# A gated cross-attention block with top-1 experts: feature-major queries with LayerNorm's factor applied behind the product, and bias plus row maximum fused per head

## The chip, the cores and the metric

One NeuronCore of a Trainium2 chip. The metric is the device time of one execution in microseconds (us), lower is better. All arithmetic is in float32.

## The reference

128 sequences of 128 tokens with 256 features, 16 heads of 16 features. `bias` is a full score bias of 128 x 16 x 128 x 128 values, which is most of the memory traffic.

```
q  = lora(layernorm(x), Wq, bq, Aq, Bq)          # layernorm without affine part, eps 1e-5
k, v = lora(ctx, ...), lora(ctx, ...)
p  = softmax(q * 16**-0.5 @ k.T + bias)          # per sequence and head
x  = x + tanh(g_xattn) * (p @ v)
y  = layernorm(x)
e  = argmax(softmax(y @ Wg + bg))                # one of 8 experts per token
x  = x + tanh(g_ffn) * (gelu(y @ W1[e] + b1[e]) @ W2[e] + b2[e])
```

## The kernel before

It has two stages. The attention stage handles one sequence per step, in a software pipeline: the step of sequence n computes scores of n, finishes n-1 and n-2, and prepares sequences up to n+6. Each engine runs its own program (SP for loads, TensorE = PE, ScalarE = ACT, VectorE = DVE, GpSimd = POOL), in program order, and the engines meet by semaphores. Work that goes by pairs of sequences alternates: in an even step PE makes the query product for the pair n+2, n+3 (I call it a *query step*), in an odd step the key product for n+1, n+2 (a *key step*). Every fourth step adds the router's work for four sequences. The last stage runs the experts over tiles of 256 tokens and has no part in the change.

What one step does before the change, by engine:

- DVE: for each quarter of the 16 heads it adds the bias to the scores, from PSUM, into `sc` (`add_bias`, L1023, 128x512 elements); after two quarters a reduction over `sc` gives eight negated row maxima (`row_max`, L1029). Then, for the sequence n-2, the reciprocal of the softmax sums (L1119), the scaling of the output (L1123) and the residual (L1130); and the statistics of both LayerNorms (L1039 with L1052 for sequence n+5, L1044 with L1052 for n-2). In every fourth step `pick_experts` runs before the bias additions (L1057 to L1070), and in the step after it `list_slots` (L1075 to L1081).
- POOL: adds the negated maxima to `sc` in two halves (`subtract_max`, L455), makes `(var+eps)**-0.5` (L477, L479) and the shift `-mean*factor` for both norms (L484, twice), adds the value bias to `x_sb` (L492) and scatters a finished sequence (L510).
- ACT: exponentials (L862), the copy of the output (L856), both LayerNorms as one activation each (`normalise`, L849), evacuation of queries, keys, values and of two transposes (L829, L840, L904, L910, L917).
- PE: scores (L560), in key steps of every fourth kind the router product (L632), p @ v (L595), the transposes of the exponent's argument (`turn`, L585, in two groups of eight), of the output (L660), the query or key product (`project`, L611), the value product (L710), the transposes of the second norm's result (L724) and of the first's (L734), which give `XT`, the moving operand of the query product.

The semaphore `s_used` counts DVE's finished quarters. PE waits for the first two before the query or key product, since both write the banks of the scores (`b_s[0]`, `b_s[1]`), for the third before the value product (`b_v` is `b_s[2]`) and for the fourth before L724. Before its next scores PE waits only for ACT's evacuations and for `s_used` of the step before. The queries are evacuated by ACT out of `b_s[0:2]` within the query step. SP issues, in each step and in this order: the context of a pair in every second step (L357), x of sequence n+6 (L364), which waits for `x2_ok` (L1130), and two halves of the bias of n+3 (L373), which wait for the last transposes of n-1.

## Time and profile before

| | |
|---|---|
| median of 3 runs | 1283.33 us (1281.91 to 1287.55) |
| span of the profiled execution | 1282.7 us, by which all sums here are made |
| attention stage | from about 18 us to about 1004 us: 128 steps |
| busy of the span | PE 99%, DVE 86%, POOL 81%, ACT 67% |
| DMA | 263.5 MB, 205 GB/s |

In the profile L12 is line 12 of the kernel. PEld is the loading of weights into TensorE, which overlaps its products; the ends of products are modelled, so the starts of the weight loads say more of PE's pace than its busy share does. Several instructions of a kind that follow each other are merged to one row with a count.

### The profile page before, as it was taken

What the parts mean: (1) busy time and instruction counts of PE and PEld (TensorE: products, weight loads), DVE (VectorE), ACT (ScalarE), POOL (GpSimd) and SP (SyncE); (2) the same over time, 40 slices, a digit from 0 to 9 for tenths busy, and PEclk for the clock granted to TensorE, in tenths of its full rate; (3) what the DMA queues carried; (4) which work ended last, traced back from release to release, by engine and by line L of the source; (5) the groups of instructions that cost most, each with busy time, mean ns of one, the idle gap of its engine ahead of it and who ended that gap; (6) DMA issues with size and microseconds to landing.
All of it is one profiled execution on the core that took longest, in us unless ns stands there. A gap on an engine that the chain in (4) does not pass through costs nothing. (4 is left out here: it accounts for less than half of the span.)

```text
span 1282.7 us, 42229 instructions
## 1 busy us (share of the span) xinstructions
PE 1264.4 (99%) x12820; PEld 1078.7 (84%) x12820; DVE 1098.7 (86%) x2504; ACT 860.4 (67%) x1916; POOL 1034.5 (81%) x1179
## 2 busy tenths in 40 slices
PE   8999999999999999999999999999999999999997
PEld 7888888888888888888888888888887788888886
DVE  6899999999999999999999999999999856665655
ACT  4777777777777777777777777777776533333332
POOL 4879989999999999999999999989988755544545
PEclk9999999999999999999999999999999999999999
DMA  6655655556655656555555555555655589888885
GB/s 237 213 179 196 193 187 181 188 186 196 191 185 181 186 187 197 191 192 183 181 185 187 195 193 185 181 184 187 192 195 182 187 271 282 281 278 281 276 281 184
DMA packets 110649, 263.48 MB, mean 205 GB/s; under 512 B 15332, under 2 KB 34278, under 8 KB 110464
## 3 DMA queue, kind: packets, MB, share of 16 engines
q1 hardware_dynamic: 96912, 226.76, 56.6%
q0 software_dynamic: 12624, 34.62, 6.9%
q10 hardware_dynamic: 1056, 1.39, 0.3%
q8 instruction: 28, 0.46, 0.2%
q14 instruction: 29, 0.24, 0.1%
HBM read 226.72 MB, written 36.91 MB: 206 GB/s over the span
## 5 line engine op out<-in xcount | busy, mean ns | idle before, releaser
L455 POOL TENSOR_TENSOR sc<-sc,negmax 128x1024 f32<-128x1024 f32 x256 | 482.4, 1901 | 25.6 <-DVE negmax L1029 20.7
L1023 DVE TENSOR_TENSOR sc<-bank,sc 128x512 f32<-128x512 f32 x512 | 328.2, 683 | 12.3 <-PE bank L560 7.5
L1029 DVE TENSOR_REDUCE negmax<-sc 128x8 f32<-128x1024 f32 x256 | 312.4, 1220 | 16.3
L862 ACT ACTIVATE PT<-bank 128x512 f32<-128x512 f32 x512 | 281.1, 607 | 1.7 <-PE bank L585 1.5
L585 PE MATMUL bank<-cst,sc 128*128 128x128 f32 x2048 | 272.6, 276 | 0.0
L585 PEld LDWEIGHTS bank<-cst,sc 128*128 128x128 f32 x2048 | 225.3, 140 | 25.8 <-issue 25.1
L525 POOL DMA_INDIRECT out<-og,ids x120 | 118.8, 990 | 114.7 <-issue 106.6
L856 ACT COPY OT<-bank 128x512 f32<-128x512 f32 x128 | 75.1, 587 | 152.1 <-PE bank L595 152.0
L510 POOL DMA_INDIRECT rows_dram<-x2n,slot_i x128 | 136.5, 1066 | 29.3 <-issue 25.2
L560 PE MATMUL bank<-KT,QT 32*128 32x256 f32 x2048 | 146.6, 400 | 0.6 <-ACT V L904 0.6
L595 PE MATMUL bank<-PT,V 128*32 128x128 f32 x4096 | 137.6, 275 | 0.3 <-issue 0.3
L710 PE MATMUL bank<-wv,CT 128*128 128x256 f32 x512 | 134.3, 385 | 0.0
L595 PEld LDWEIGHTS bank<-PT,V 128*32 128x32 f32 x4096 | 106.6, 110 | 32.1 <-ACT PT L862 27.2
L611 PE MATMUL bank<-XT,wq 128*128 128x256 f32 x512 | 125.3, 388 | 2.9 <-DVE sc L1023 2.4
L611 PE MATMUL bank<-CT,wk 128*128 128x256 f32 x512 | 125.6, 388 | 0.9 <-DVE sc L1023 0.9
L840 ACT ACTIVATE KT<-bank,bk_half,cst 128x256 f32<-128x256 f32 x256 | 123.9, 565 | 1.5 <-PE bank L611 1.5
L763 PE MATMUL bank<-xgT,w_sb 128*128 128x256 f32 (+1 forms) x552 | 123.1, 366 | 0.4 <-DMA w_sb<-in_w 0.3
L777 PE MATMUL bank<-CT,hT 128*128 128x256 f32 x516 | 122.6, 379 | 0.7 <-DVE og L1238 0.7
L560 PEld LDWEIGHTS bank<-KT,QT 32*128 32x128 f32 x2048 | 92.5, 184 | 25.0 <-issue 21.2
L1238 DVE SCALAR_TENSOR_TENSOR og<-bank,tg,QT 128x512 f32<-128x512 f32 x64 | 45.9, 717 | 78.2 <-DMA out<-og,ids 56.6
L710 PEld LDWEIGHTS bank<-wv,CT 128*128 128x128 f32 x512 | 94.2, 191 | 19.9 <-DVE sc L1023 5.3
L777 PEld LDWEIGHTS bank<-CT,hT 128*128 128x128 f32 x516 | 97.1, 190 | 13.8 <-issue 1.1
(148 smaller groups left out, 2052.0 us busy)
## 6 DMA issues: line engine op xcount, KB each, us to landing
sc<-in_bias SPq DMA_DIRECT2D x256, 512.0 KB, 4.9
w_sb<-in_w SPq DMA_DIRECT2D x69, 257.0 KB, 3.9
CT<-in_w SPq DMA_DIRECT2D x69, 256.0 KB, 4.1
xg<-rows_dram SPq DMA_DIRECT2D x63, 272.0 KB, 3.8
x_sb<-in_x SPq DMA_DIRECT2D x128, 128.0 KB, 2.0
CT<-in_ctx_in SPq DMA_DIRECT2D x64, 256.0 KB, 5.4
rows_dram<-x2n,slot_i POOLq DMA_INDIRECT x128, 3.8
out<-og,ids POOLq DMA_INDIRECT x120, 4.0
```

Source lines behind the costliest of these rows:

```text
L455: nc.gpsimd.tensor_tensor(s, s, m, ALU.add).then_inc(sub_ok, 1)
L510: nc.gpsimd.indirect_dma_start(rows_dram, bass.IndirectOffsetOnAxis(ap=slot_i[:, g, j:j + 1], axis=0), x2n[:, t.slot(8), :], None).then_in ...
L560: ins = mm(b_s[j][:, 2 * P * c:2 * P * c + 2 * P], QT[rows, pair, c, P * sq:P * sq + P], KT[rows, pair, c, sq].rearrange("p e k -> p (e k) ...
L585: ins = nc.tensor.transpose(turn_bank(t, q)[:, P * h:P * h + P], sc[:, t.slot(4), o:o + P], ident)
L595: ins = mm(b_x[CELL * j:CELL * j + CELL, P * (h // 4):P * (h // 4) + P], V[:, t.slot(8), h, :], PT[:, t.slot(2), P * h:P * h + P], start=T ...
L611: ins = mm(b_s[o][:, 0:2 * P], W[w][:, c, o * P:o * P + P], moving[:, c, :], start=(c == 0), stop=(c == KC - 1))
L710: ins = mm(b_v[:, 0:HID], CT[:, pair, c, tok:tok + P], W["v"][:, c, :], start=(c == 0), stop=(c == KC - 1))
L777: ins = mm(y_half, hT[:, t.slot(2), c, a * P:a * P + P], w2_of(t)[:, c * HID:c * HID + HID], start=(c == 0), stop=(c == KC - 1))
L840: ins = nc.scalar.activation(KT[:, pair, o, :, e, :], b_s[o][:, 0:2 * P].rearrange("p (s k) -> p s k", s=2), ACT.Identity, bias=bk_half[:, ...
L862: nc.scalar.activation(PT[:, t.slot(2), 512 * q:512 * q + 512], turn_bank(t, q)[:], ACT.Exp).then_inc(pt_ready, 1)
L1023: nc.vector.tensor_tensor(s, b_s[q][:], s, ALU.add).then_inc(s_used, 1)
L1029: nc.vector.tensor_reduce(negmax[:, t.slot(2), 8 * h:8 * h + 8], sc[:, t.slot(4), 1024 * h:1024 * h + 1024].rearrange("p (h k) -> p h k", ...
```

## The change

1. The query product takes raw x, laid out feature-major by the host (`x_turned`) and loaded into `XT` by one DMA per pair. The first `normalise`, the PE transposes L734 and the copy L917 go. The subtraction of the mean is folded into the query weights at set-up (each weight column less its mean). LayerNorm's factor, one number per token, is multiplied in behind the product: SP writes POOL's column of 128 factors to DRAM (`send_scale`) and reads it back as a row spread over 128 partitions (`spread_scale`) into `RS`; DVE multiplies the product by `RS` into `QT` (`scale_queries`), and ACT adds the query bias in place.
2. Bias addition and row maximum become one `tensor_tensor_reduce` per head on DVE, 128x128 elements with an accumulated maximum, 16 per step. POOL subtracts the maxima.
3. The value product moves to bank `b_x`, so its wait for `s_used` goes. PE waits for `scaled_ok` before the scores of a key step. POOL makes one shift instead of two.

```diff
@@ sync
+            def send_scale(t):
+                sp.wait_ge(rs_ok, t.n(1, 1))
+                sp.dma_start(rs_dram[t.n()], ln[:, (t.k - 7) % 8, 0, 0:1]).then_inc(rs_out, 16)
+            def spread_scale(t):
+                if t.reached(4):
+                    sp.wait_ge(scaled_ok, t.per(2, 1, -1))
+                sp.wait_ge(rs_out, t.n(16, 16))
+                sp.dma_start(RS[:, pair, tok:tok + P], rs_rows[t.n()].partition_broadcast(P)).then_inc(rs_in[pair], 16)
             def step(i, k):
+                behind = seq(i, k, -4)
+                if behind and not (isinstance(i, int) and k < 0):
+                    send_scale(behind)
...
-                        sp.wait_ge(xn_ok, t.n(1, -7))
+                if behind and behind.slot(2) == 0:
+                    if behind.reached(4):
+                        sp.wait_ge(q_ready, behind.per(2, KC, -KC))
+                    sp.dma_start(XT[:, behind.k // 2 % 2], x_turned[behind.per(2)]).then_inc(xT_in[behind.k // 2 % 2], 16)
+                if behind:
+                    spread_scale(behind)
@@ gpsimd
-                nc.gpsimd.tensor_tensor(s, s, m, ALU.add).then_inc(sub_ok, 1)
+                nc.gpsimd.tensor_tensor(s, s, m, ALU.subtract).then_inc(sub_ok, 1)
@@ tensor
                 if cur:
                     pe.wait_ge(v_evac, val.n() if val else N)
+                    if ky and ky.slot(2) == 0:
+                        pe.wait_ge(scaled_ok, ky.per(2, 1, 1))
...
-                    if cur:
-                        pe.wait_ge(s_used, cur.n(4, 3))
-                    elif val.reached(1):
+                    if not cur and val.reached(1):
...
-                if nxt:
-                    pe.wait_ge(xn_ok, nxt.n(1, 1))
-                    for c in range(KC):
-                        ins = nc.tensor.transpose(b_x[:, c * P:c * P + P],
-                                                  xn[:, nxt.slot(2), c * P:c * P + P], ident)
-                    ins.then_inc(xt_ready, 1)
@@ scalar, queries(t), now the last work of a query step
+                act.wait_ge(scaled_ok, t.per(2, 1, 1))
                 for o in range(KC):
-                    act.wait_ge(q_ready, t.per(2, KC, o + 1))
-                    ins = nc.scalar.activation(QT[:, pair, o, :], b_s[o][:, 0:2 * P],
+                    ins = nc.scalar.activation(QT[:, pair, o, :], QT[:, pair, o, :],
                                                ACT.Identity, bias=bq_col[:, o:o + 1])
@@ vector
                 dve.wait_ge(s_ready, t.n(4, q + 1))
-                s = sc[:, t.slot(4), 512 * q:512 * q + 512]
-                nc.vector.tensor_tensor(s, b_s[q][:], s, ALU.add).then_inc(s_used, 1)
-            def row_max(t, h):
-                nc.vector.tensor_reduce(
-                    negmax[:, t.slot(2), 8 * h:8 * h + 8],
-                    sc[:, t.slot(4), 1024 * h:1024 * h + 1024].rearrange("p (h k) -> p h k", h=8),
-                    AX.X, ALU.max, negate=True).then_inc(max_ok, 1)
+                for h in range(4 * q, 4 * q + 4):
+                    s = sc[:, t.slot(4), P * h:P * h + P]
+                    ins = nc.vector.tensor_tensor_reduce(
+                        out=s, in0=b_s[q][:, P * (h % 4):P * (h % 4) + P], in1=s, scale=1.0, scalar=LOWEST,
+                        op0=ALU.add, op1=ALU.max, accum_out=rowmax[:, t.slot(2), h:h + 1])
+                ins.then_inc(s_used, 1)
...
+            def scale_queries(t):
+                dve.wait_ge(rs_in[pair], t.per(4, 32, 32))
+                for o in range(KC):
+                    dve.wait_ge(q_ready, t.per(2, KC, o + 1))
+                    ins = nc.vector.tensor_tensor(QT[:, pair, o, :], b_s[o][:, 0:2 * P], RS[:, pair, :], ALU.mult)
+                ins.then_inc(scaled_ok, 1)
@@ vector, step: behind L1130 and ahead of L1044
+                        if qry and qry.slot(2) == 0:
+                            scale_queries(qry)
@@ vector, set-up: behind merge(2, "k")
+            dve.wait_ge(s_setc, 1)
+            nc.vector.scalar_tensor_tensor(
+                out=W["q"][:], in0=bank[SETUP_BANKS[1]][:, 0:HID].unsqueeze(1).broadcast_to([P, KC, HID]),
+                scalar=-1.0 / HID, in1=W["q"][:], op0=ALU.mult, op1=ALU.add).then_inc(s_setd, 1)
```

## Rows read from the trace of the kernel before

**Rows 1.** The page, part 1: busy us (share of the span) and instructions by engine.
```profile
PE 1264.4 (99%) x12820; PEld 1078.7 (84%) x12820; DVE 1098.7 (86%) x2504; ACT 860.4 (67%) x1916; POOL 1034.5 (81%) x1179
```
**Rows 2.** Busy time in four consecutive steps: stage, length, busy, clock, DMA share, GB/s.
```profile
500.55:508.66 8.11, 8.11 (x103) 7.03 (x103) 7.60 (x16) 6.47 (x16) 7.56 (x9) 1.00 0.54 170
508.66:516.26 7.60, 7.60 (x88) 6.49 (x87) 7.18 (x16) 5.46 (x13) 6.79 (x9) 1.00 0.65 208
...
sum 30.85, PE 30.85 PEld 26.15 DVE 28.75 ACT 23.58 POOL 28.07; mean PE 7.71 PEld 6.54 DVE 7.19 ACT 5.90 POOL 7.02
```
**Rows 3.** Timeline of PE's weight loads: start, duration, then the idle time before.
```profile
508.66 0.74 PEld L560 LDWEIGHTS bank<-KT,QT 32*128 32x128 f32 x16 [0.17 <-issue]
...
514.97 0.25 PEld L734 LDWEIGHTS bank<-cst,xn 128*128 128x128 f32 x2
515.18 0.90 PEld L585 LDWEIGHTS bank<-cst,sc 128*128 128x128 f32 x8
516.26 0.74 PEld L560 LDWEIGHTS bank<-KT,QT 32*128 32x128 f32 x16 [0.17 <-issue]
...
529.03 0.73 PEld L710 LDWEIGHTS bank<-wv,CT 128*128 128x128 f32 x4 [0.22 <-DVE sc L1023]
```
**Rows 4.** Timeline of DVE over the same steps.
```profile
499.54 0.25 DVE L1119 RECIPROCAL rden<-bank 128x16 f32<-128x16 f32 x1
...
501.71 1.29 DVE L1023 TENSOR_TENSOR sc<-bank,sc 128x512 f32<-128x512 f32 x2
...
508.90 0.19 DVE L1057 TENSOR_REDUCE lmax<-L 128x4 f32<-128x32 f32 x1
...
510.54 1.29 DVE L1023 TENSOR_TENSOR sc<-bank,sc 128x512 f32<-128x512 f32 x2
...
515.63 0.25 DVE L1119 RECIPROCAL rden<-bank 128x16 f32<-128x16 f32 x1
...
516.53 0.42 DVE L1130 TENSOR_TENSOR x<-bank,x_sb 128x256 f32<-128x256 f32 x1
517.05 0.43 DVE L1044 BATCH_NORM_STATS2 st<-x 128x6 f32<-128x256 f32 x1
...
518.28 1.28 DVE L1023 TENSOR_TENSOR sc<-bank,sc 128x512 f32<-128x512 f32 x2
```
**Rows 5.** The page, part 5: groups by line, count, busy us, mean ns.
```profile
L1023 DVE TENSOR_TENSOR sc<-bank,sc 128x512 f32<-128x512 f32 x512 | 328.2, 683 | 12.3 <-PE bank L560 7.5
L1029 DVE TENSOR_REDUCE negmax<-sc 128x8 f32<-128x1024 f32 x256 | 312.4, 1220 | 16.3
```
**Rows 6.** Timeline of DVE in the set-up: small instructions with no input.
```profile
16.92 0.07 DVE L1001 MEMSET terms<- 128x18 f32 x1
16.94 0.07 DVE L1002 MEMSET upto<- 128x9 f32 x1
```
**Rows 7.** Timeline of an early step in which DVE waits for the scores.
```profile
31.86 0.74 PEld L560 LDWEIGHTS bank<-KT,QT 32*128 32x128 f32 x16 [0.17 <-issue]
...
33.10 0.69 DVE L1023 TENSOR_TENSOR sc<-bank,sc 128x512 f32<-128x512 f32 x1 [1.00 <-PE bank L560]
```
**Rows 8.** Timeline of POOL: the same instruction in two consecutive steps.
```profile
521.64 3.75 POOL L455 TENSOR_TENSOR sc<-sc,negmax 128x1024 f32<-128x1024 f32 x2
...
526.71 0.50 POOL L484 TENSOR_SCALAR x2n<-x2n,mv 128x1 f32<-128x1 f32 x2 [0.18 <-POOL x2n L479]
...
529.18 3.75 POOL L455 TENSOR_TENSOR sc<-sc,negmax 128x1024 f32<-128x1024 f32 x2
```
**Rows 9.** Timeline of SP's DMA issues.
```profile
508.41 0.33 SPq L364 DMA_DIRECT2D x_sb<-in_x  x1
509.06 0.85 SPq L373 DMA_DIRECT2D sc<-in_bias  x2
```
**Rows 10.** The page, part 6: DMA issues, count, KB each, us to landing.
```profile
sc<-in_bias SPq DMA_DIRECT2D x256, 512.0 KB, 4.9
...
x_sb<-in_x SPq DMA_DIRECT2D x128, 128.0 KB, 2.0
```
**Rows 11.** Timeline of the start-up, PE's weight loads and DVE.
```profile
10.95 0.69 DVE L991 SCALAR_TENSOR_TENSOR wk<-bank,wk 128x512 f32<-128x512 f32 x1
...
11.40 1.59 PEld L611 LDWEIGHTS bank<-XT,wq 128*128 128x128 f32 x8 [0.76 <-ACT XT L917]
```

More of the change, by code:

```diff
@@ L39 @@
 TO_FT = float(3 << 30)
+LOWEST = -3.4028234663852886e38
 CELL = 32
@@ L548, in _ @@
             pe.wait_ge(s_id, 16)
+            pe.wait_ge(s_cst, 16)
+            pe.wait_ge(s_setd, 3)
+            for c in range(KC):
+                ins = mm(bank[SETUP_BANKS[1]][:, 0:HID], cst[:, C_ONE:C_ONE + P], W["q"][:, c, :],
+                         start=(c == 0), stop=(c == KC - 1))
+            ins.then_inc(s_setc, 1)
             def scores(t):
@@ L843, in keys, with normalise @@
                 ins.then_inc(k_evac, 1)
-            def normalise(t, n, row, rows, dst, done, turned):
-                act.wait_ge(shift_ok[n], t.n(1, 1))
+            def normalise(t):
+                row = t.slot(8)
+                act.wait_ge(shift_ok, t.n(1, 1))
                 if t.reached(2):
-                    act.wait_ge(turned, t.n(1, -1))
-                nc.scalar.activation(dst, rows, ACT.Identity, bias=ln[:, row, n, 1:2],
-                                     scale=ln[:, row, n, 0:1]).then_inc(done, 1)
+                    act.wait_ge(x2t_ready, t.n(1, -1))
+                nc.scalar.activation(xn2[:, row, :], x2[:, t.slot(2), :], ACT.Identity, bias=ln[:, row, 1, 1:2],
+                                     scale=ln[:, row, 1, 0:1]).then_inc(xn2_ok, 1)
             def copy_output(t):
@@ L1135, in step @@
                     aggregate(ahead, 0)
+                if qry and qry.slot(2) == 0 and not done:
+                    scale_queries(qry)
                 stats(done, 1)
```

110 lines of the change are left out of this document (52 added, 58 removed).

## The prediction

> **What bounds the kernel now.** I read the busy shares first: PE 99%, DVE 86%, POOL 81% [rows 1]. In the page's slices DVE stands at nine tenths until the expert stage begins and falls then, so the change acts on the attention stage alone: 128 steps, 32 groups of four. One group, at the full clock, takes 30.85 us [rows 2]. Then the timelines, to see who has slack. PE's weight loads follow each other densely; what is idle before them is 0.17 to 0.33 us at changes of tile shape, and one wait of 0.22 us for DVE in the group [rows 3]. DVE is just as dense: from the reciprocal to the next step's first bias addition is 2.17 us of instructions and their own hand-overs, and bias plus maximum takes 510.54 to about 515.6, 5.0 us [rows 4]. POOL's own round is 521.64 to 529.18, 7.54 us, against a mean step of 7.71 [rows 2, 8]. ACT has room: 5.90 of 7.71 [rows 2]. So three engines lie within about 2.5%. PE sets the pace, DVE has nearly nothing to spare, and POOL is next. Whatever the change takes from PE is gained only if DVE does not become slower by more than a few tenths per step.
>
> **PE.** Two transposes per step go. From the load of L734 to the next load is 514.97 to 515.18, 0.21 to 0.22 us [rows 3]; four times 0.22 is 0.88 us a group. PE's floor becomes 30.85 - 0.88 = 29.97 us. The 0.22 us wait [rows 3] disappears with the value product's new bank; I don't count it, since new waits of such a size are likely, and keep 29.75 as the lower end. Both products that stay wait for DVE's first two quarters as before.
>
> **DVE, the fused instruction.** Per step, four additions and two reductions of 4 x 683 + 2 x 1220 ns [rows 5], 5.0 us as they overlap, give way to 16 instructions of 128x128. Everything hangs on T, the time from start to start of two of them. No row shows this instruction. A neighbour with the same operands lasts 683 ns at 512 columns and 0.42 us at 256 [rows 4, 5], so about 1.03 ns a column and 0.287 us at 128 columns. Two additions with no wait between them take 1.28 us, where 2 x 0.683 would be 1.37 [rows 4, 5]: some 0.08 us of each hides under the next. That gives 0.205 us. Writing the accumulated maximum is a further small operation. Its nearest row is the memset, which has an output and no input and starts 0.02 us after the one before [rows 6]. I take T = 0.235 us. The lower end is 0.205 (the maximum for nothing). The upper end is no overlap and a full separate operation of the size of the router's smallest, 0.19 us [rows 4]: 0.48 us. I take the low value since the instructions have no waits between them, like the pair of additions, and the write is nearest to the memset. At that value the block takes 16T = 3.8 us instead of 5.0.
>
> The Trainium skill speaks on both terms. "VectorE: DVE Perf Modes", section "Two Vector instructions with no wait between them", counts an operation that writes out its accumulator as two instructions, of which the second has no input; no row here shows one, and by it there are 32 instructions in place of 16. The same page's "The DRAIN you can't avoid" and "Rules for kernel authors" say that the next operation doesn't begin until the pipe is empty, advise against fusing for speed and ask for a low count of operations. Against that stands this trace's overlap of 0.08 us in a pair [rows 4, 5]. By the rule the fused block would be the slower one; that is the first rival.
>
> **DVE, the scaling.** Once per pair, between L1130 and L1044, two 128x256 multiplications from PSUM come in, each 0.42 us like L1130, starting 0.34 us apart (0.42 - 0.08). They fill the hand-over between L1130 and L1044, 517.05 - 516.53 = 0.52 us, so they add about 0.6 us per pair. What is queued behind the wait for `q_ready` and `rs_in` on DVE is the statistics and then the next bias block. The query product is done long before L1130 ends, since the product lies before the value product, L724, L734 and L585 in PE's order.
>
> **The new meeting point.** PE may start the scores of a key step only when DVE has scaled. Before, DVE could trail by up to two us. So I cost pairs, from the scores of one key step to those of the next. The first bias instruction can begin 33.10 - 31.86 = 1.24 us after the scores' first load [rows 7]. In the query step, from the reciprocal to the end of scaling is (516.53 - 515.63) + 0.34 + 0.34 + 0.42 = 2.0 us [rows 4], 2.1 with the wake-up. The router's choice costs 510.54 - 508.90 = 1.6 us [rows 4] in one pair of two.
> - Pair with the router's work (8.11 + 7.60 us before [rows 2]): PE needs 15.71 - 0.44 = 15.27. The way through DVE is 1.24 + 16T + 2.17 + 1.6 + 16T + 2.1 = 7.1 + 32T: 14.6 at T = 0.235.
> - The other pair (30.85 - 15.71 = 15.14 before [rows 2]): PE needs 14.70. The way through the key step on PE and the query step on DVE is 7.39 + 1.24 + 16T + 2.1 = 10.7 + 16T: 14.5 at T = 0.235.
>
> Both stay under PE's time until T = 0.25, but only just. PE then sets the pace, with 29.97 us a group.
>
> **The rest, costed at nothing.** POOL loses one L484 in two, 0.25 us of 0.50 [rows 8], so its round is 7.3 us against a step of 7.49: covered, by 0.2 us, and it caps any further gain at 29.2 a group. ACT loses a normalisation and a copy. The query bias moves to the end of its query step and waits there for the scaling; behind it is queued the next step's output copy, which waits for p @ v anyway, and ACT has 1.8 us a step free [rows 2]. SP issues, per step, a 512-byte write, a spread read and half an XT load more, all ahead of the two bias loads. Its x load already waits for L1130, at 508.41, and the bias follows at 509.06 [rows 9]; 0.33 us for each issue moves the bias by under 1 us, and it has two steps of slack against 4.9 us to landing [rows 10]. The factor's write is issued at a step's start and may land behind 1 MB of bias, 4.9 us, still before that x load; the spread read goes out behind it and lands about 2 us later [rows 10], near 511 for the trace's step. The scaling that needs it comes at 516.9 [rows 4]: 5.7 us of cover. If that cover were gone, DVE would wait inside the meeting point. DMA is at 0.54 to 0.65 [rows 2] and moves some 12% more.
>
> **Start-up.** The query weights now wait for the key weights' merge, 10.95 + 0.69, one more merge and a scaling of about 1.1 us together: 12.8 instead of 11.40 [rows 11]. Scaling stands in front of the key product too. Bounds 0 and 4 us; I take 2.
>
> **The sum.** 1282.7 - 32 x 0.88 + 2 = 1256.5; the median stood 0.6 above the profiled span: 1257 us. With the wait on the value product gained too and no start-up cost: 1282.7 - 32 x 1.10 = 1247.5.
>
> **The rivals.**
> 1. *The fused instructions don't overlap.* T is then 0.287 or more, with a write that waits for its result 0.30 to 0.34. From T = 0.25 each further 0.01 us costs 0.48 us a group, and from T = 0.27 on the kernel is slower than before: 16.3 + 15.3 = 31.6 at 0.287, which gives 1309. At 0.30: 16.7 + 15.5 = 32.2, and 32 x 1.35 + 2 more than 1283: 1328. At 0.34: 18.0 + 16.4, 1397 (there the second pair goes through DVE twice, 5.5 + 32T). For it: a running maximum has to be complete before it is written, and no row shows such an instruction. Against: the pair of additions, the memsets. At the upper end, 0.48, it would be some 1680; I leave that out, since it stacks two worst cases. Chance 32%.
> 2. *PE's gain is spent at the meeting point.* With T of 0.255 to 0.275, or 0.3 to 0.4 us more of wake-ups per pair, the cycles through DVE take the 0.44 us per pair back: about 1282. For it: the two margins above are 0.2 and 0.7 us. Chance 14%.
> 3. *The factor comes late.* It decides when the round trip through DRAM exceeds about 8 us, from a step's start to 516.9. Two us too late would cost each of 64 pairs 2 us: 1385. The cover speaks against it. Chance 4%.
>
> **How the numbers follow.** The forecast case (PE sets the pace, 1247 to 1268) has 50%. Faster by over 0.5% is that case, 0.50; within 0.5%, about what a measurement of this kernel can tell from no change, is rival 2, 0.14; slower is rivals 1 and 3, 0.36, the other sign. The range reaches from the lower end, 1247, to 1360 (T about 0.32), which leaves out roughly the upper half of rival 1 and of rival 3. The likeliest case's own range is 1247 to 1268.
>
> **What would show it.** Right: 2048 fused instructions on DVE that start 0.22 to 0.25 us apart; L1023 and L1029 gone; a bias block of 3.6 to 4.0 us; DVE busy well under nine tenths of the attention stage; PE dense, with a group near 30 us and no wait for DVE before L560. Wrong: PE idle before L560 in key steps behind DVE's multiplication (rival 1 or 2, told apart by the start-to-start time), DVE idle before the multiplication behind a DMA into RS (rival 3), or SP's bias issues so late that DVE waits for them.

## The result, and the profile after

The changed kernel takes 2017.83 us (median of 4 runs, 2013.23 to 2019.98); the kernel before took 1284.24 beside it. The ratio is 1.570 [1.567, 1.574]. The prediction said 1257, between 1247 and 1360: the sign is wrong, and the range is missed by 658 us. The profiled execution has a span of 2016.1 us.

Page of the changed kernel: busy time by engine (answers [rows 1]), the chain that ended last, four groups of part 5 (count | busy us, mean ns | idle before, releaser), and one DMA issue (KB, us to landing).

```profile
PE 1390.3 (69%) x12568; PEld 1158.6 (57%) x12568; DVE 974.1 (48%) x5961; ACT 772.7 (38%) x1660; POOL 997.8 (49%) x1051
...
DMA 69%; PE 14%; SPq 9%; issue 6%; DVE 1%; ACT 0%; POOLq 0%; POOL 0%; DVEq 0%; ACTq 0%
...
L1042 DVE CUSTOM_DVE_ANT_0 sc<-bank,sc 128x128 f32<-128x128 f32 x2048 | 443.9, 286 | 264.3 <-PE bank L595 133.7
...
L595 PE MATMUL bank<-KT,QT 32*128 32x256 f32 x2048 | 195.6, 509 | 476.0 <-DVE QT L1101 443.9
...
L1052 DVE BATCH_NORM_STATS2 st<-x_sb 128x6 f32<-128x256 f32 x128 | 53.7, 419 | 399.6 <-DMA x_sb<-in_x 399.5
...
L1042 DVE DVE_READ_ACCUMULATOR2_ANT rowmax<- 128x1 f32 x2048 | 170.1, 83 | 0.3 <-issue 0.2
...
x_sb<-in_x SPq DMA_DIRECT2D x128, 128.0 KB, 11.1
```

No engine is the bound any more: PE fell from 99% to 69%, DVE from 86% to 48%. The chain is DMA for 69% of the span, and nearly all of that is one transfer: the next row of the page gives `rs_dram<-x2n`, the factor's write, 68%. PE is idle for 476 us ahead of the scores (L595), 444 of them behind DVE's scaling; DVE waits 400 us for x. The same 128 KB load of x that landed in 2.0 us [rows 10] takes 11.1. Who waits for the write is told by the waits of SP's queue from 100 to 1700 us (total us, times, longest) and by its issues in two steps (start, duration):

```profile
SPq L364 <- DMA rs_dram<-x2n: 1085.4, 117, 11.8
```

```profile
802.80 0.86 SPq L402 DMA_DIRECT2D sc<-in_bias  x2
804.38 0.36 SPq L356 DMA_DIRECT2D rs_dram<-x2n  x1
805.07 0.35 SPq L379 DMA_DIRECT2D CT<-in_ctx_in  x1
805.74 0.33 SPq L384 DMA_DIRECT2D x_sb<-in_x  x1
806.39 0.33 SPq L389 DMA_DIRECT2D XT<-in_x_turned  x1
815.20 0.33 SPq L366 DMA_DIRECT2D RS<-rs_dram  x1
815.87 0.86 SPq L402 DMA_DIRECT2D sc<-in_bias  x2
816.96 0.83 SPq L356 DMA_DIRECT2D rs_dram<-x2n  x1
818.04 0.58 SPq L384 DMA_DIRECT2D x_sb<-in_x  x1
828.73 0.33 SPq L366 DMA_DIRECT2D RS<-rs_dram  x1
829.38 0.86 SPq L402 DMA_DIRECT2D sc<-in_bias  x2
```

Each step has the same shape. SP issues the write (804.38), the loads of x, and then waits at L364 for the write to land, 10.8 us after its issue; only then go the spread read, the two bias loads and the next step's write, 1.8 us together. The next round is 816.96 to 828.73, 11.8 us. SP's own loop is 12.6 us long from the write at 804.38 and 13.5 from spread read to spread read (815.20 to 828.73), and the steps are 13.33 us apart in the mean (first score weight load of the first step at 37.57, of the 128th at 1730.4, over 127). In the kernel before they were 7.71 [rows 2]. They are not even: over steps 17 to 112, intervals of 17.1 and 9.6 us alternate in the mean, since PE waits for the scaling once in a pair, and two of SP's rounds go to a pair. The bias loads, which had nothing to do with the factor, stand behind its wait. The DMA engines don't carry a load meanwhile; their busy tenths in 40 slices of 815 to 829 us:

```profile
DMA  0009772893799489999997722000200000000000
```

From about 824 to 828.7 they are all but idle, while SP waits for the landing of the 512 bytes that it issued at 816.96. A window of 700 to 800 us (length; busy us and count of PE, PEld, DVE, ACT, POOL; granted clock, DMA share, GB/s):

```profile
700.00:800.00 100.00, 69.71 (x696) 57.66 (x696) 48.64 (x338) 42.00 (x90) 53.64 (x56) 0.80 0.60 128
```

The granted clock is 0.80 here, a mean of its two levels, where [rows 2] show full speed; a score product takes 509 ns in the mean instead of 400. PE is idle for 30 of the 100 us and waits for others, so I count the clock as a consequence of the waits and not as their cause; that is argued. `e2_no_factor_dma` below, without the factor's route, has a granted clock of 0.996 in the mean.

The fused instruction is as the prediction had it. DVE in one step (start, duration, the idle time before in brackets):

```profile
809.41 0.29 DVE L1042 CUSTOM_DVE_ANT_0 sc<-bank,sc 128x128 f32<-128x128 f32 x1 [1.05 <-PE bank L595]
809.63 0.08 DVE L1042 DVE_READ_ACCUMULATOR2_ANT rowmax<- 128x1 f32 x1
809.63 0.29 DVE L1042 CUSTOM_DVE_ANT_0 sc<-bank,sc 128x128 f32<-128x128 f32 x1
...
812.98 0.26 DVE L1137 RECIPROCAL rden<-bank 128x16 f32<-128x16 f32 x1
```

Two instructions per head, 286 and 83 ns, and the next head starts 0.21 us after the first: the 83 ns are hidden, and so is a part of the 286. Sixteen heads take 3.57 us to the reciprocal.

### The profile page after: what moved, and what is told of

It reads as the page before. It is cut to its first block, busy times and chain, and to the rows that moved or that the text cites. A ratio compares the mean times of both kernels' runs of the same rounds, so it can differ in the third digit from the quotient of the medians.

```text
span 2016.1 us, 45866 instructions
## 1 busy us (share of the span) xinstructions
PE 1390.3 (69%) x12568; PEld 1158.6 (57%) x12568; DVE 974.1 (48%) x5961; ACT 772.7 (38%) x1660; POOL 997.8 (49%) x1051
## 4 chain that ended last, share of the span: by engine, by line
DMA 69%; PE 14%; SPq 9%; issue 6%; DVE 1%; ACT 0%; POOLq 0%; POOL 0%; DVEq 0%; ACTq 0%
DMA rs_dram<-x2n 68%; PE bank L788 6%; PE bank L802 6%; SPq L402 5%; SPq L366 2%; PE bank L776 1%; DMA x_sb<-in_x 1%; DMA RS<-rs_dram 1%; DVE sc L1042 1%; SPq L356 0%; PE bank L595 0%; PE bank L629 0%; PE bank L620 0%; SPq L384 0%; SPq L379 0%
## 5 line engine op out<-in xcount | busy, mean ns | idle before, releaser
L1042 DVE CUSTOM_DVE_ANT_0 sc<-bank,sc 128x128 f32<-128x128 f32 x2048 | 443.9, 286 | 264.3 <-PE bank L595 133.7
L484 POOL TENSOR_TENSOR sc<-sc,rowmax 128x1024 f32<-128x1024 f32 x256 | 480.0, 1896 | 156.9 <-DVE rowmax L1042 148.7
L595 PE MATMUL bank<-KT,QT 32*128 32x256 f32 x2048 | 195.6, 509 | 476.0 <-DVE QT L1101 443.9
L595 PEld LDWEIGHTS bank<-KT,QT 32*128 32x128 f32 x2048 | 119.7, 238 | 511.5 <-DVE QT L1101 373.3
L886 ACT ACTIVATE PT<-bank 128x512 f32<-128x512 f32 x512 | 281.6, 604 | 17.6 <-PE bank L620 14.1
L1052 DVE BATCH_NORM_STATS2 st<-x_sb 128x6 f32<-128x256 f32 x128 | 53.7, 419 | 399.6 <-DMA x_sb<-in_x 399.5
L852 ACT ACTIVATE QT<-QT,cst 128x256 f32<-128x256 f32 x128 | 58.0, 501 | 444.8 <-DVE QT L1101 444.8
L645 PEld LDWEIGHTS bank<-XT,wq 128*128 128x128 f32 x512 | 106.5, 219 | 135.1 <-issue 113.8
L629 PE MATMUL bank<-PT,V 128*32 128x128 f32 x4096 | 178.6, 330 | 0.3 <-ACT PT L886 0.3
L1042 DVE DVE_READ_ACCUMULATOR2_ANT rowmax<- 128x1 f32 x2048 | 170.1, 83 | 0.3 <-issue 0.2
L924 ACT COPY V<-bank 128x256 f32<-128x256 f32 x128 | 48.3, 377 | 286.9 <-PE bank L745 286.9
L1101 DVE TENSOR_TENSOR QT<-bank,RS 128x256 f32<-128x256 f32 x128 | 49.1, 419 | 196.1 <-DMA RS<-rs_dram 191.3
## 6 DMA issues: line engine op xcount, KB each, us to landing
x_sb<-in_x SPq DMA_DIRECT2D x128, 128.0 KB, 11.1
```

The source lines that it names most:

```text
L484: nc.gpsimd.tensor_tensor(s, s, m, ALU.subtract).then_inc(sub_ok, 1)
L595: ins = mm(b_s[j][:, 2 * P * c:2 * P * c + 2 * P], QT[rows, pair, c, P * sq:P * sq + P], KT[rows, pair, c, sq].rearrange("p e k -> p (e k) ...
L629: ins = mm(b_x[CELL * j:CELL * j + CELL, P * (h // 4):P * (h // 4) + P], V[:, t.slot(8), h, :], PT[:, t.slot(2), P * h:P * h + P], start=T ...
L645: ins = mm(b_s[o][:, 0:2 * P], W[w][:, c, o * P:o * P + P], moving[:, c, :], start=(c == 0), stop=(c == KC - 1))
L886: nc.scalar.activation(PT[:, t.slot(2), 512 * q:512 * q + 512], turn_bank(t, q)[:], ACT.Exp).then_inc(pt_ready, 1)
L1042: ins = nc.vector.tensor_tensor_reduce(out=s, in0=b_s[q][:, P * (h % 4):P * (h % 4) + P], in1=s, scale=1.0, scalar=LOWEST, op0=ALU.add, op ...
```

## Experiments

Ratios are to the kernel before, run beside each kernel on the same chip: it took 1283.3 to 1284.4 us there, and 1296.6 where that is said. A single run has no interval. Lines of a diff that count for nothing are left out.

### Each part alone

`e1_fused_only`: the kernel before, with all 16 heads fused.

```diff
-                s = sc[:, t.slot(4), 512 * q:512 * q + 512]
-                nc.vector.tensor_tensor(s, b_s[q][:], s, ALU.add).then_inc(s_used, 1)
+                for h in range(4 * q, 4 * q + 4):
+                    ins = nc.vector.tensor_tensor_reduce(
...
-                    row_max(cur, 0)
-                    row_max(cur, 1)
```

> The kernel before with only the fused bias and row maximum (and POOL subtracting). In the changed kernel two fused instructions start 0.211 us apart, so a block of 16 takes 3.4 us instead of 5.0. If the fused instruction is harmless and PE set the pace before, the time is 1270 to 1284 us, since PE's own work is untouched, and DVE falls to about 70% busy. If the fused instruction had a part in the slowdown, the time is above 1290.

Measured: 1290.17 us, ratio 1.0049 [1.0033, 1.0066]: just above its expectation's line of 1290, where fusing itself costs something, 0.5% here.

`e2_no_factor_dma`: the changed kernel without the write, the spread read and SP's wait.

```diff
-                sp.wait_ge(rs_ok, t.n(1, 1))
-                sp.dma_start(rs_dram[t.n()], ln[:, (t.k - 7) % 8, 0, 0:1]).then_inc(rs_out, 16)
-                sp.wait_ge(rs_out, t.n(16, 16))
-                sp.dma_start(RS[:, pair, tok:tok + P], rs_rows[t.n()].partition_broadcast(P)).then_inc(rs_in[pair], 16)
-                dve.wait_ge(rs_in[pair], t.per(4, 32, 32))
+            nc.vector.memset(RS[:], 1.0).then_inc(s_warm, 1)
```

> The changed kernel without the round trip of the factor: RS is filled once with ones, nothing is written to DRAM or read back, and SP doesn't wait for it (LayerNorm's factor is left out of the queries). Everything else stays: turned x, the multiplication on DVE, PE's wait for it. If the round trip alone is the slowdown, the time falls to what the prediction had for PE setting the pace, 1247 to 1268 us. If the meeting point of PE and DVE costs too, it stays above 1284.

Measured: 1271.76 us, ratio 0.9898 [0.9882, 0.9915], between the two cases of its expectation. All of the loss, 746 us, sits in the factor's way through DRAM; everything else of the change gains 1%.

`e3_send_only`: `e2_no_factor_dma` with the write and SP's wait back. `e4_spread_only`: the same with the spread read alone, from the first line of x.

```diff
+                sp.dma_start(rs_dram[t.n()], ln[:, (t.k - 7) % 8, 0, 0:1]).then_inc(rs_out, 16)
+                sp.wait_ge(rs_out, t.n(16, 16))
```

```diff
+                sp.dma_start(RS[:, pair, tok:tok + P], x_line[t.n()].partition_broadcast(P)).then_inc(rs_in[pair], 16)
```

> As the run without the round trip, but SP still writes the 128 factors to DRAM in each step and waits for that write before the bias loads; the read back is gone (factor left out). If the write is slow by itself, as in the start-up, where 9.5 us pass from its issue to the next issue with no bias in flight, a step stays at 11 us or more and the time is 1700 to 2000. If the write only waits behind the spread read and 1 MB of bias, it lands some 3 us earlier and the time is below 1600.

> As the run without the round trip, but in each step a row of 128 values is read from DRAM to 128 partitions into RS, out of x instead of the factors, with no write before it and no wait for one (factor replaced by other numbers). DMA moves little for some 3 us behind each such read in the changed kernel. If the read is only a load on the DMA engines, it fits in the 40% that is free and the time is 1250 to 1300; if it holds up the bias loads, over 1350.

Measured, one run each: 1828.29 us with the write, 1280.01 with the spread read. The write is 557 us of the 746. The read costs 8 us by itself. Behind the write it is worth 190, 1.5 us a step, because then its issue and hand-over lie in SP's serial round.

`e5_unfused`: the whole changed kernel, with the four additions and two reductions of before.

```diff
-                    ins = nc.vector.tensor_tensor_reduce(
...
+                nc.vector.tensor_tensor(s, b_s[q][:], s, ALU.add).then_inc(s_used, 1)
```

> The changed kernel with the bias addition and row maximum of the kernel before, everything else as changed. If the round trip sets the step, the time is the changed kernel's, 1990 to 2040 us. If the fused instruction had a part in the slowdown beside it, it falls below 1950.

Measured: 2028.27 us in one run (before: 1296.57). The ratio is 1.564, against 1.570 with the fused heads. A bias block 1.4 us longer in each step changes nothing, steps stay at 13.30 us. The fused instruction has no part in the slowdown.

### What makes the write slow

All of these are `e3_send_only` with another form of the write. `e7_wide_send` writes 512 bytes per partition, 64 KB. `e8_spaced_send` writes the same 128 pieces of 4 bytes, 512 bytes apart. `e9_split_send` writes them packed, as four transfers of 32 partitions. The wide write takes its data from `RS` (ones).

```diff
+                sp.dma_start(rs_wide[t.n()], RS[:, 0, 0:P]).then_inc(rs_out, 16)
```

```diff
+                sp.dma_start(rs_wide[t.n()][:, 0:1], ln[:, (t.k - 7) % 8, 0, 0:1]).then_inc(rs_out, 16)
```

```diff
+                for g in range(4):
+                    sp.dma_start(rs_dram[t.n()][32 * g:32 * g + 32], ln[32 * g:32 * g + 32, (t.k - 7) % 8, 0, 0:1]).then_inc(rs_out, 16)
```

> As the run with the write alone (1828 us), but the write carries 512 bytes from each of 128 partitions (64 KB) instead of 4 bytes from each (it writes ones to a scratch area; factor left out). If the time comes from writing to DRAM and waiting for it behind the bias loads, nothing changes: 1750 to 1900. If it comes from the 4-byte pieces, the write lands within 5 to 6 us, beside the wait that SP has anyway, and the time is 1270 to 1350.

> As the run with the write alone (1828 us), but the 128 pieces of 4 bytes go to places 512 bytes apart in DRAM instead of side by side in one stretch of 512 bytes (factor left out). If the pieces hinder each other because they share a line in DRAM, the time falls below 1450; if a piece of 4 bytes is slow wherever it goes, or if all pieces go through one DMA engine, it stays at 1750 to 1900.

> As the run with the write alone (1828 us), but in four DMAs of 32 partitions each, issued one after the other and waited for together (factor left out). If one DMA's pieces are worked off one after the other while others could run beside it, the landing shrinks from about 10 us to some 4 to 5 and the time falls below 1450. If the pieces of all DMAs queue behind each other, it stays at 1800 or rises by the issues, 4 x 0.35 us a step.

Measured, one run each: 1279.33 us wide, 1275.92 spaced, 1756.7 split. Then the distance was varied: `e13_send_64b` and `e14_send_8b` put the pieces 64 and 8 bytes apart (the 16 in the diff is a 2 in the latter).

```diff
+        rs_pad = nc.dram_tensor("rs_pad", (N, P, 16), F32, kind="Internal").ap()
+                sp.dma_start(rs_pad[t.n()][:, 0:1], ln[:, (t.k - 7) % 8, 0, 0:1]).then_inc(rs_out, 16)
```

> The write alone (factor left out), its 128 pieces of 4 bytes 64 bytes apart, so that 8 of them fall into each 512 bytes. In the start-up the second write has only 128 KB in front of it: 7.9 us to the next issue with 128 pieces in 512 bytes, 5.4 with 64, 1.75 with one. If each piece that shares a stretch costs some 50 ns, one after the other, it is 2.0 to 2.4 us here and the time 1270 to 1285. If any sharing makes it slow, it is above 4 us and the time above 1350.

> The write alone (factor left out), its pieces 8 bytes apart, 64 in 512 bytes, without the read of 1 KB per partition that the run with that spacing had (1579 us). If the price goes by the pieces in a stretch, the second write takes 5 to 5.7 us again, the landing behind the bias is some 3 us less than with pieces side by side (10.5), and the time is 1350 to 1500. If the 1579 us came from the larger read, it is below 1320.

Measured, one run each (before: 1296.55): 1287.56 us at 64 bytes, 1425.57 at 8 bytes. Both expectations missed in the start-up, on the fast side: 1.8 us for 2.0 to 2.4, and 3.5 for 5 to 5.7.

The landing is also read from a quiet place. In the start-up SP issues its second write behind one 128 KB load and then waits for it; the time to its next issue is the landing and the hand-over. SP's issues there, in `e3_send_only`, `e9_split_send`, `e14_send_8b`, `e13_send_64b`, `e8_spaced_send`, `e7_wide_send`, in this order:

```profile
15.96 0.39 SPq L356 DMA_DIRECT2D rs_dram<-x2n  x1
23.88 0.80 SPq L401 DMA_DIRECT2D sc<-in_bias  x2
```

```profile
15.27 1.77 SPq L357 DMA_DIRECT2D rs_dram<-x2n  x4
25.08 0.83 SPq L402 DMA_DIRECT2D sc<-in_bias  x2
```

```profile
12.86 0.39 SPq L357 DMA_DIRECT2D rs_pad<-x2n  x1
16.39 0.80 SPq L402 DMA_DIRECT2D sc<-in_bias  x2
```

```profile
11.50 0.38 SPq L357 DMA_DIRECT2D rs_pad<-x2n  x1
13.30 0.80 SPq L402 DMA_DIRECT2D sc<-in_bias  x2
```

```profile
11.97 0.39 SPq L357 DMA_DIRECT2D rs_wide<-x2n  x1
13.72 0.80 SPq L402 DMA_DIRECT2D sc<-in_bias  x2
```

```profile
11.63 0.39 SPq L359 DMA_DIRECT2D rs_wide<-RS  x1
13.43 0.80 SPq L404 DMA_DIRECT2D sc<-in_bias  x2
```

| pieces | apart | in 512 bytes | issue to next issue | kernel, ratio to before |
|---|---|---|---|---|
| 128 of 4 bytes | 4 | 128 | 7.9 us | 1.42 |
| the same in four transfers | 4 | 128 | 9.8 us | 1.37 |
| 128 of 4 bytes | 8 | 64 | 3.5 us | 1.10 |
| 128 of 4 bytes | 64 | 8 | 1.8 us | 0.99 |
| 128 of 4 bytes | 512 | 1 | 1.75 us | 0.99 |
| 128 of 512 bytes | 512 | 1 | 1.8 us | 1.00 |

With the pieces 512 bytes apart, neither the bytes (512 or 64 K) nor the size of a piece (4 or 512 bytes) matters. What matters is how closely the pieces lie in DRAM. Packed side by side they land 6 us later than 64 bytes apart. Splitting the transfer doesn't shorten the landing (9.8 us); the kernel gains 4% by it. That the pieces of one small stretch wait for each other is what this pattern suggests. How long such a stretch is, no run shows: the third column counts by 512 bytes, but by 64 bytes it would be 16, 16, 8, 1, 1, 1 pieces, which fits as well. A fixed price for each piece that shares a stretch doesn't fit: halving them takes 6.1 us above the floor of 1.8 down to 1.7.

The traces do show where the time is not. These are the DMA engines in `e3_send_only` from 15.9 to 23.9 us and in `e13_send_64b` from 11.4 to 13.4 us, in 40 slices each (busy tenths; packets), the same load of x and the same write:

```profile
DMA  0009944520000000000000000000000000000000
DMA packets 288, 0.13 MB, mean 16 GB/s; under 512 B 160, under 2 KB 288, under 8 KB 288
```

```profile
DMA  0000000000000599346599999641000000000000
DMA packets 288, 0.13 MB, mean 66 GB/s; under 512 B 160, under 2 KB 288, under 8 KB 288
```

The 288 packets are the same, and the last is over at 17.7 us in the one and at 12.8 in the other, 1.7 and 1.3 us after the write's issue. SP goes on 6.2 us after that in the packed form, and 0.5 us after it with 64 bytes between. So the late landing is behind the packets that the profile records, and not in the DMA engines' busy time; what goes on there, in the memory or on the way to it, no run shows.

The Trainium skill, "DMA: Bandwidth & Descriptors", section "Specifications", says that a piece under 512 bytes is done as a read-modify-write. By itself that doesn't give these times, as pieces of 4 bytes 512 bytes apart land in 1.75 us; it would agree with them if such writes of one stretch had to follow each other, which is argued and not shown.

`e10_stride2` is the whole changed kernel with the factors 8 bytes apart and a spread read of 1 KB rows; `e11_stride2_half` is the same with 8 heads fused.

```diff
-        rs_dram = nc.dram_tensor("rs_dram", (N, P, 1), F32, kind="Internal").ap()
+        rs_dram = nc.dram_tensor("rs_dram", (N, P, 2), F32, kind="Internal").ap()
-        RS = sb("RS", [P, 2, 2 * P])
+        RS = sb("RS", [P, 2, 2 * P, 2])
```

> The changed kernel with one difference in the round trip: the factors lie 8 bytes apart in DRAM instead of 4, so that the destination of the write is no longer one unbroken stretch; the spread read brings 1 KB instead of 512 bytes to each partition and DVE reads every second value. Theory 1 (an unbroken destination makes one slow transfer of 128 pieces, worked off in one place): the write lands in about 5 us as with pieces 512 bytes apart, and the time is 1278 to 1300. Theory 2 (pieces that share a stretch of DRAM hinder each other): they still share it, and the time stays above 1800.

> The same with the fused instruction for eight of sixteen heads, as in the run of that kind on the kernel before. If theory 1 holds, the stall of DVE once in 8 steps goes too and the time is 10 to 15 us under the run before it: 1265 to 1285, under both kernels. Under theory 2 it stays above 1800.

Measured: 1578.89 us, ratio 1.2208 [1.2165, 1.2252], and three runs of 1576.83 to 1591.07, ratio 1.2264 [1.2221, 1.2307] (before: 1296.57). Both theories of the expectation missed, by some 280 and 220 us: the gap of a word is no cure, and it isn't without effect either. The kernel with half the heads fused isn't faster here, as SP's round sets the step. One word of spacing gives back 0.35 of 0.57, in the real kernel too, and steps fall from 13.33 to 9.78 us. It isn't enough, and a wider spacing makes the spread read larger in proportion (64 bytes would be 1 MB a step), so I found no form of this route that beats the kernel before. A read back of single words out of a wider spacing wasn't tried. In the start-up of `e10_stride2` the second write takes 5.4 us to the next issue (13.29 to 18.68, the figure in the expectation of `e13_send_64b`), against 3.5 in `e14_send_8b`: there a spread read of 128 KB stands in front of it.

### Why the rest of the change gains only 1%

`e1_fused_only` is slower than before though its bias block is shorter. Two lines of its DVE timeline in sequence, and the weight load of PE that is late by it:

```profile
526.74 0.18 DVE L1051 BATCH_NORM_AGGREGATE mv<-st 128x2 f32<-128x6 f32 x1
530.10 0.29 DVE L1028 CUSTOM_DVE_ANT_0 sc<-bank,sc 128x128 f32<-128x128 f32 x1 [3.17 <-issue]
```

```profile
531.93 1.59 PEld L612 LDWEIGHTS bank<-XT,wq 128*128 128x128 f32 x8 [1.00 <-DVE rowmax L1028]
```

Once per round of the loop (8 steps) DVE stands still for 3.2 us, and "issue" says that nothing visible holds it. From 100 to 900 us the waits count 11 of them, up to 3.3 us, 35.3 us in all; before had 11 of at most 0.4, 4.5 us in all. Along with it goes the page's row of the DMA queue of kind "instruction" (packets, MB), here of `e6_half_fused`, where 8 heads are fused, and of `e16_fused_12`, with 12:

```profile
q14 instruction: 33, 0.27, 0.1%
```

```profile
q14 instruction: 92, 0.75, 0.2%
```

The kernel before has 29 packets and `e1_fused_only` 93, of 8 KB each. The kernels fall into two classes, without exception: 29 to 35 packets and no stop (0, 8 heads fused), 91 to 96 packets and the stop (12, 16 heads). When the packets move says more. From 200 to 880 us, all inside the loop, the kernel before moves none and `e6_half_fused` one; `e1_fused_only` moves 55 in 11 rounds, five a round. One of the five falls into each stop. These are the instruction queue's rows of `e1_fused_only` from 200 to 880 us and from 526.9 to 530.2:

```profile
q14 instruction: 55, 0.45, 0.2%
```

```profile
q14 instruction: 1, 0.01, 0.8%
```

In all eleven stops of `e1_fused_only` between 215 and 842 us that packet starts 0.9 to 1.1 us after the stop begins, and 0.9 to 1.2 us in those of `e2_no_factor_dma`, `e18_no_scale_full`, `e15_no_dma_12` and `e16_fused_12` in the loop. And the place is always one: the stop lies ahead of the bias additions of every eighth step, the third of the round, and that is the step with which the body of DVE's loop begins in the kernel (`run_steps(dve, ...)` has 12 rounds, from step 18 on, and `e2_no_factor_dma` has 12 such stops). The two classes, the packet in each stop and the place are measured; that the packets carry DVE's program is argued, as the profile doesn't say whose they are.

Four kernels, `e2_no_factor_dma` and three more, separate the stop from the new meeting point. `e12_no_dma_half` is `e2_no_factor_dma` with 8 heads fused (no stop, meeting point kept). `e17_no_scale_half` and `e18_no_scale_full` take out the scaling on DVE and PE's wait for it as well, with 8 and 16 heads fused.

```diff
-                    if ky and ky.slot(2) == 0:
-                        pe.wait_ge(scaled_ok, ky.per(2, 1, 1))
-                        if qry and qry.slot(2) == 0:
-                            scale_queries(qry)
```

> The changed kernel without the round trip (factor left out, 1272 us with all heads fused) and with eight heads fused. PE waited some 1.5 us once in 8 steps behind DVE's stall, 15 rounds. If that stall is all that keeps it from the prediction's 1257 us, the time is 1247 to 1260. If the slower DVE block (about 4.2 us instead of 3.4) costs more at the meeting point, it stays at 1265 to 1275.

> The changed kernel without the round trip and without the multiplication on DVE: ACT takes the queries out of PSUM and adds their bias, as before the change, and PE waits for no scaling (LayerNorm's factor is left out of the queries). Eight heads are fused, so that DVE's program stays small. PE has 0.88 us a group less to do and nothing that the profile shows to wait for. If the prediction's floor for PE is right, the ratio to before is 0.972 to 0.982. If POOL's own round (7.3 us a step) or ACT holds it, 0.983 to 0.995.

> The same with all sixteen heads fused, so that DVE's stall of 3.3 us once in 8 steps is back. If the stall costs what PE waits in its step (1.0 to 1.5 us in each of 15 rounds), the ratio is 0.012 to 0.018 above the run before it; if DVE's shorter block makes up for the stall, both are equal within 0.003.

`e6_half_fused` is the kernel before with 8 of 16 heads fused; `e15_no_dma_12` and `e16_fused_12` are `e2_no_factor_dma` and the kernel before with 12 (`q >= 3` in the diff).

```diff
+                if q >= 2:
+                    s = sc[:, t.slot(4), 512 * q:512 * q + 512]
+                    nc.vector.tensor_tensor(s, b_s[q][:], s, ALU.add).then_inc(s_used, 1)
+                    return
```

> The kernel before with the fused instruction for eight of the sixteen heads; the other eight keep two bias additions and one reduction. With all heads fused, DVE stood still for 3.2 to 3.4 us with no wait in the profile once in every 8 steps, which is one round of the unrolled loop, and the instruction queue moved 93 packets instead of 29. Theory 1 (DVE's program for one round has outgrown what is held, and is fetched again): half the extra instructions give shorter stalls or none, packets near 29 to 60, and a time of 1275 to 1284 us. Theory 2 (the stall comes with the kind of instruction): the stall stays 3.2 us and the time stays at 1288 to 1292.

> The changed kernel without the round trip (factor left out), twelve heads fused, four with one addition and one reduction. DVE's block is about 12 x 0.211 + 0.68 + 0.6 = 3.8 us, against 3.4 with all fused (ratio to before 0.990) and 4.2 with eight (0.997). By the prediction's pair formulas DVE then stays just under PE. If the stall goes with the smaller program, the ratio is 0.975 to 0.985. If the stall is still there, 0.988 to 0.995.

> The kernel before with twelve heads fused. With eight it was 0.994 of before and had no stall, with sixteen 1.005 and stalls. Without a meeting point a shorter DVE block gives nothing more once PE sets the pace: 0.992 to 0.996 if the stall is absent, 0.997 to 1.006 if it is there.

Four of these expectations missed. `e12_no_dma_half` took 1292.11 us, above both its ranges, and its ratio of 0.9968 is above them too. `e15_no_dma_12` and `e16_fused_12` are slower than the worst that was named. `e18_no_scale_full` is 0.0117 above `e17_no_scale_half`, a hair under its 0.012 to 0.018.

The steps are read from the starts of PE's score weight loads; for `e17_no_scale_half`:

```profile
500.62 0.75 PEld L590 LDWEIGHTS bank<-KT,QT 32*128 32x128 f32 x16 [0.32 <-issue]
508.00 0.74 PEld L590 LDWEIGHTS bank<-KT,QT 32*128 32x128 f32 x16 [0.17 <-issue]
515.23 0.74 PEld L590 LDWEIGHTS bank<-KT,QT 32*128 32x128 f32 x16 [0.17 <-issue]
522.46 0.74 PEld L590 LDWEIGHTS bank<-KT,QT 32*128 32x128 f32 x16 [0.17 <-issue]
530.35 0.74 PEld L590 LDWEIGHTS bank<-KT,QT 32*128 32x128 f32 x16 [0.17 <-issue]
```

530.35 - 500.62 = 29.73 us for four steps. Averaged in this way over steps 17 to 112 by their place in the loop's round, in us (the third place is the one with the stop):

| kernel | heads fused | steps of the round | round | ratio, 95% interval |
|---|---|---|---|---|
| before | 0 | 7.60 7.60 7.55 8.11 7.60 7.71 7.45 8.11 | 61.7 | 1 |
| e6_half_fused | 8 | 7.60 7.45 7.45 8.11 7.60 7.45 7.45 8.11 | 61.2 | 0.9943 [0.9924, 0.9962] |
| e16_fused_12 | 12 | 7.91 7.81 8.72 8.11 7.60 7.45 7.45 8.11 | 63.2 | 1.0177 [1.012, 1.0233] |
| e1_fused_only | 16 | 7.60 7.45 8.43 8.11 7.60 7.45 7.45 8.11 | 62.2 | 1.0049 [1.0033, 1.0066] |
| e17_no_scale_half | 8 | 7.47 7.23 7.23 7.89 7.39 7.23 7.23 8.05 | 59.7 | 0.9785 [0.9762, 0.9808] |
| e18_no_scale_full | 16 | 7.38 7.23 8.47 7.89 7.38 7.23 7.23 8.05 | 60.9 | 0.9902 [0.9883, 0.9922] |
| e12_no_dma_half | 8 | 7.67 7.23 7.79 7.89 7.59 7.25 7.46 8.04 | 60.9 | 0.9968 [0.9954, 0.9983] |
| e15_no_dma_12 | 12 | 7.48 7.27 9.38 7.93 7.44 7.26 7.43 8.04 | 62.2 | 1.0068 [1.004, 1.0095] |
| e2_no_factor_dma | 16 | 7.39 7.23 8.64 7.89 7.38 7.23 7.23 8.04 | 61.0 | 0.9898 [0.9882, 0.9915] |

The times are 1278.24, 1322.63, 1290.17, 1256.5, 1270.08, 1292.11, 1304.7, 1271.76 us from the second row down; before took 1284.4, 1296.55, 1284.28, 1283.3, 1283.3, 1296.57, 1296.55 and 1284.28 beside them.

What follows:
- The stop costs PE 1.0 to 1.4 us of its 3.2 (8.43 against 7.45, 8.47 against 7.23, 8.64 against 7.23): DVE's slack takes up the rest. By `e17_no_scale_half` and `e18_no_scale_full` it is worth 1.2% of the kernel, 14 us.
- Three means hold a round unlike the others. In `e1_fused_only`, `e18_no_scale_full` and `e15_no_dma_12` the first of the twelve rounds has no stop in the third place; without it the first two are 8.52 and 8.58.
- The meeting point costs nothing with 16 heads fused: `e2_no_factor_dma` and `e18_no_scale_full` have equal steps to 0.01 us but for the stop. With 8, where the block takes 4.25 us (the first fused head at 503.11, the reciprocal at 507.36), it costs 1.2 us a round, 1.0 without one step of 10.49 us; the ratios put it at 1.8% of the kernel, but before took 1296.57 beside the one and 1283.3 beside the other. In `e12_no_dma_half` PE is seen waiting for DVE's multiplication ahead of the scores, 27 times in some 53 steps between 300 and 700 us:

```profile
PEld bank L593 <- DVE QT L1111: 10.5, 27, 0.5
```

- So the two ways of avoiding trouble exclude each other. Half fused avoids the stop and pays at the meeting point; fully fused does the reverse.
- Twelve heads were meant as the way between, and both kernels missed: they have the stop, and lose more by it. In `e15_no_dma_12` the step with the stop takes 9.38; in `e16_fused_12` the two steps ahead of it are longer as well (7.91, 7.81). Why this is so with 12 and not with 16 stays open.
- `e6_half_fused` beats both kernels, the one before by 0.6%. It leaves nothing out; it has the shorter bias block and no other part of the change.

## Why the prediction was wrong

**The step that failed is "The rest, costed at nothing".** It took the factor's way from the landing of other transfers, at most the 4.9 us of the bias for the write and "about 2 us" for the read [rows 10], asked whether the spread reached `RS` before the scaling, and found 5.7 us of cover. Two things in it are wrong.
- *The size.* The write was priced only by the bias that it may land behind, and nothing was put down for itself. The write is 512 bytes and takes 10.8 to 11.8 us beside other work, 7.9 in the start-up. No row of the kernel before shows a write of small pieces side by side into DRAM, and its cost had to be bounded from both sides; I gave it the time of loads and nothing above.
- *The place.* The cover was counted at the scaling, on DVE. But SP waits for the write in its own order, and all it issues behind that wait is late with it. "0.33 us for each issue moves the bias by under 1 us" priced the issues and left out the wait between them. The text asked what DVE has queued behind its new wait, and not what SP has. It is the spread, both bias loads and the next write, so the landing comes once in every step: 128 times, not 64. SP stands at L364 for 9.3 us a step in the mean (1085.4 / 117); all the cover is its own issues behind the write.

**Rival 3, the factor comes late,** had the right transfer at 4%. Its condition was met: the write alone exceeds its 8 us. Its price failed: two us too late in 64 pairs, 1385. A wait inside SP's round makes that round the period of every step; in the rival's own terms the pair came 11.3 us late (2 x 13.33 - 2 x 7.70) and not 2. From the first step's scores to the 128th's are 1730.4 - 37.57 = 1692.8 us, against 995.55 - 17.63 = 977.9 in the kernel before: 714.9 us. The start-up adds 37.57 - 17.63 = 19.9, and the rest of the kernel gives back 1.5; together they are the 733.4 us between the two spans.

**Start-up: +2.** With the factor's route left out the first scores begin at 19.56 us instead of 17.63: +1.9 for 2. That they agree is in part luck: the first scores begin at 17.66, 18.56 and 20.13 in `e6_half_fused`, `e1_fused_only` and `e16_fused_12`, which have the set-up of before, and at 18.86 and 21.17 in `e18_no_scale_full` and `e17_no_scale_half`. With the route they begin at 37.57, since the first two writes stand in the start-up as well.

**Rival 1, no overlap, 32%,** is refuted. T is 0.211 us; the forecast took 0.235 between 0.205 and 0.48. The method held (slope from a neighbour of the same operands, overlap from a pair of additions, the write from a memset): 286 ns measured, 287 worked out. The rule of the Trainium skill that I weighed, "VectorE: DVE Perf Modes", section "Two Vector instructions with no wait between them", that an instruction which writes out its accumulator is two, is confirmed by the 2048 rows of the second kind. The same page's "The DRAIN you can't avoid" says that the next doesn't begin until the pipe is empty, and adds that one which isn't held starts earlier. This trace agrees with the second: 0.211 us from start to start, with 286 + 83 ns of work. The advice against fusing came true with 12 and 16 heads (1.018 and 1.005) and not with 8 (0.994), and what goes with the loss is the stop in the loop and not the pipe.

**Rival 2, PE's gain is spent at the meeting point, 14%.** It doesn't happen at the real T, and the formulas were good. At 16T = 3.4 they give 13.9 and 14.1 us against PE's 15.27 and 14.70: no cost; measured are at most (61.03 - 60.88) / 2 = 0.08 us a group, nearly all of it in the step with the stop. With the 4.25 us block they give 15.6 and 14.95: 0.33 + 0.25 = 0.58 us a group. Measured: (60.92 - 59.72) / 2 = 0.60, or 0.48 without the one step of 10.49 us.

**PE: -0.88 us a group, floor 29.97.** `e17_no_scale_half` has 59.72 / 2 = 29.86 us a group, between the floor and its lower end, 29.75. `e2_no_factor_dma` without its stop has (61.03 - 1.41) / 2 = 29.81.

**What no step named** is the stop. The forecast less the factor's route should have been `e2_no_factor_dma`: 1257 forecast, 1271.8 measured. The stop came 12 times in that trace, once in each round of DVE's loop, and cost PE 1.41 us: 1271.8 - 12 x 1.41 = 1254.9. The sum of the other terms was therefore right to about 2 us, which is less than the start-up alone scatters. The fused heads' 32 instructions of each step, in place of six, were priced by their time on the engine, and never by their number in the loop.

So had the write landed like a load, the change would have gained 1% at most: with the whole route left out the ratio is 0.990, with a spaced write alone 0.993, and the read alone costs 8 us. Whether it can be brought off SP's path (another queue, or the spread and its wait behind the bias loads) wasn't tried; as x, issued right behind the write, takes 11.1 us to land too, moving the wait alone need not be enough.

## What to carry to other kernels

Price a DMA that writes DRAM by how closely its small pieces lie, not by its bytes; 128 words side by side in DRAM took longer than 1 MB of bias [rows 10]. Where a queue waits for one transfer, write down all that it issues behind that wait, for the landing then enters the period of the loop and no cover elsewhere helps. When an edit trades few instructions for many, look at how long the loop's program becomes, in the rows of the instruction queue, beside what the instructions cost.

## What the runs showed of the hardware beyond that

- 128 writes of 4 bytes to DRAM take 7.9 us side by side, 3.5 at 8 bytes apart, 1.8 at 64 or 512 bytes apart, while the recorded packets of all these forms are over 1.3 to 2.2 us after the issue.
- With 24 or 32 fused-head instructions a step, DVE stops for 3.1 to 3.5 us once in a round of 8 steps, at the head of its loop, and the instruction queue moves five packets of 8 KB a round, one of them within the stop; with 16 or none there is no stop, and next to no packets move in the loop.
- The kernel before took 1% longer beside eight of the kernels (1296.6 us), and their traces show where. In all eight, SP's four filling writes between the two stages start over 10.7 to 10.9 us, and ACT and DVE stand still meanwhile; in the kernel before and the other kernels they start over 3.6 to 4.6 us. The row is of `e16_fused_12`, waits between 980 and 1100 us. Why is open; a ratio nearly leaves it out.

```profile
ACT hT L945 <- remote: 8.4, 1, 8.4
```
